# Typed graph attention: GpSimd builds the one-hots of the weighted sums, and one stage divides, turns and projects

## The reference, cut to what matters

```python
def _L1_gnn_ref(h, ..., a_linears, ..., skip, node_type, etype, row_idx, col_idx):
    ...
    ex = jnp.exp(score - m[col_idx])
    denom = jax.ops.segment_sum(ex, col_idx, num_segments=n)
    alpha = ex / denom[col_idx]
    agg = jax.ops.segment_sum(alpha[..., None] * msg_edge, col_idx, num_segments=n)
    agg = agg.reshape(n, OUT_DIM)
    out = _typed_matmul(agg, a_linears, node_type)
    out = jax.nn.sigmoid(skip)[node_type][:, None] * out
    return out
...
x = x + _L1_gnn_ref(_layernorm(x, axis=-1), ...)
```

## Time and profile before

| | |
|---|---|
| median of three runs | 5765.59 us |
| the profiled execution's span | 6191.8 us |
| `build_counts`, 536.4 to 870.1 | 333.7 us |
| `edge_weights`, 3168.1 to 3272.4 | 104.3 us |
| `edge_sums`, 3274.8 to 3503.7 | 228.9 us |
| division, to the end of its stage, 3503.7 to 3513.6 | 9.9 us |
| turn and loading, 3513.6 to 3528.4 | 14.8 us |
| four projections, 3528.4 to 3624.9 | 96.5 us |

### The profile page before, as it was taken

The page is one execution under the profiler, slowest core; times in us unless marked ns, Lnnn a source line. Parts: engine busy times, 40 slices in busy tenths (PEclk is TensorE's granted clock), DMA queues, the critical chain, the costliest instruction groups (busy, mean ns, idle before and its releaser), DMA issues. The chain is left out here.

```text
span 6191.8 us, 76002 instructions
## 1 busy us (share of the span) xinstructions
PE 4533.9 (73%) x22806; PEld 3190.3 (52%) x22842; DVE 3374.5 (55%) x7236; ACT 1645.9 (27%) x3766; POOL 2414.1 (39%) x2719
## 2 busy tenths in 40 slices
PE   5877978757758694566558889998999495354468
PEld 1223434545546452444436677777888363344456
DVE  8988972645556654677757743342111333544454
ACT  0964652411213251011100133333222121100022
POOL 0851018545540534555500028861122301577710
PEclk8988989868878897666758989999999697677779
DMA  0002447422232388777746410004333332233310
GB/s 31 2 11 102 190 181 210 157 45 39 41 60 79 100 322 277 236 246 240 242 132 218 149 25 12 17 7 129 100 110 120 91 100 61 91 91 90 92 29 21
DMA packets 413215, 696.03 MB, mean 112 GB/s; under 512 B 116843, under 2 KB 301299, under 8 KB 408203
## 3 DMA queue, kind: packets, MB, share of 16 engines
q1 hardware_dynamic: 316322, 440.23, 22.7%
q0 software_dynamic: 96320, 250.79, 13.5%
q10 hardware_dynamic: 192, 0.15, 0.0%
HBM read 450.69 MB, written 239.64 MB: 111 GB/s over the span
## 5 line engine op out<-in xcount | busy, mean ns | idle before, releaser
L1109 PE MATMUL wsum_a_ps<-wsum_a_hot,wsum_a_rows 128*128 128x128 f32 x1664 | 290.4, 349 | 359.7 <-DVE big L1136 185.7
L2242 POOL DMA_INDIRECT big<-hgt_table,edge_key x416 | 394.2, 948 | 364.4 <-DVE hgt_s_tmp L2335 221.0
L1095 POOL DMA_INDIRECT wsum_a_rows<-table,edge_src x416 | 434.2, 1044 | 221.9 <-issue 165.5
L1109 PEld LDWEIGHTS wsum_a_ps<-wsum_a_hot,wsum_a_rows 128*128 128x128 f32 x1664 | 272.1, 257 | 378.0 <-issue 210.0
L3928 PE MATMUL sagel_ps<-sagel_piece,sagel_high 128*128 128x448 f32 x1050 | 399.0, 380 | 0.8 <-issue 0.8
L3928 PE MATMUL sagel_ps<-sagel_piece,sagel_low 128*128 128x448 f32 x1050 | 385.2, 367 | 0.0
L2325 DVE TENSOR_REDUCE hgt_highest<-hgt_s_pm 128x8 f32<-128x1024 f32 x208 | 253.3, 1219 | 188.3 <-remote 181.6
L2242 POOL DMA_INDIRECT big<-gat_table,own_src x288 | 272.5, 946 | 211.6 <-issue 82.0
L2292 PE MATMUL hgt_s_pq<-big 128*128 x1248 | 249.9, 372 | 136.0 <-DVE hgt_s_tmp L2335 75.6
L2282 PE MATMUL hgt_s_pm<-hgt_s_turned,pick 112*128 112x128 bf16 x1664 | 188.5, 282 | 216.9 <-DVE hgt_highest L2325 185.3
L790 PE MATMUL cnt_ps<-cnt_hot_s,cnt_hot_d 128*128 128x512 bf16 (+1 forms) x1724 | 309.8, 333 | 39.0 <-DVE cnt_hot_s L772 34.9
(11 more groups left out here) (1007 smaller groups left out, 10909.7 us busy)
## 6 DMA issues: line engine op xcount, KB each, us to landing
hgt_edge_values<-big SPq DMA_DIRECT2D x104, 512.0 KB
big<-hgt_edge_values SPq DMA_DIRECT2D x104, 512.0 KB, 4.6
x<-counts SPq DMA_DIRECT2D x75, 448.0 KB, 3.3
x<-counts SPq DMA_DIRECT2D x75, 336.0 KB, 2.9
counts<-big SPq DMA_DIRECT2D x25, 832.0 KB, 3.4
counts<-big SPq DMA_DIRECT2D x25, 768.0 KB, 3.3
big<-counts SPq DMA_DIRECT2D x30, 640.0 KB
counts_turned<-big SPq DMA_DIRECT2D x30, 640.0 KB
```

Source lines behind the costliest of these rows:

```text
L1095: nc.gpsimd.indirect_dma_start(rows[n % DEEP][:, u, :], None, table, bass.IndirectOffsetOnAxis(ap=e.src[:, g:g + 1], axis=0)).then_inc(gat ...
L1109: mm = nc.tensor.matmul(ps[r.slot % 2][u][:, k * P:(k + 1) * P], rows[r.slot][:, u, k * P:(k + 1) * P], hot[r.slot % 2][:, u, :], start=Tr ...
L2242: nc.gpsimd.indirect_dma_start(rows[n % DEEP][:, u, :], None, at.table, bass.IndirectOffsetOnAxis(ap=at.index[:, g:g + 1], axis=0)).then_i ...
```

## The change

- `edge_sums`: GpSimd builds the one-hots, one operation of 128x128 for each group (416 in all, L2964 of the new kernel) in a buffer that is free at that time. `hot` and `val` have three places. VectorE only copies the weights (L2981) and multiplies (L2983). The load of `w_a` is issued by SyncE behind the fifth step's rows.
- `typed_out` takes the place of `divide`, `turn`, the load and the four `add_projection`. It goes tile by tile: VectorE multiplies by the reciprocal (L3046), TensorE transposes (L3082), ScalarE copies out, TensorE multiplies by all four matrices (L3094), VectorE adds the four types' parts (L3061) and takes the statistics (L3065).
- `edge_weights`: three places in place of two for `hot_t` and `pd`, and one-hots made two batches ahead.
- `not_below_zero`: a bitwise AND of a register before each wait on its value, in `build_counts` (440 on VectorE, 50 on ScalarE) and `edge_sums` (416 on TensorE, 25 on ScalarE).

```diff
+def not_below_zero(value, highest):
+    return value & ((1 << highest.bit_length()) - 1)
...
@@ build_counts, VectorE @@
-                            dve.wait_ge(moved, buckets[u] + 1)
+                            dve.wait_ge(moved, not_below_zero(buckets[u], 2 * NT - 1) + 1)
...
@@ edge_weights @@
+        pd = [c.enter_context(nc.psum_tensor(f"{nm}_pd{a}", [P, 512], F32)) for a in range(RING)]
...
-                    if b >= 2:
-                        dve.wait_ge(spread, b - 1)
+                    if b >= RING:
+                        dve.wait_ge(spread, b - RING + 1)
...
                 make(0)
+                make(1)
                 for b in range(batches):
-                    if b + 1 < batches:
-                        make(b + 1)
+                    if b + 2 < batches:
+                        make(b + 2)
...
@@ edge_sums @@
-        val, hot = many(2, "val", [P, R, W]), many(2, "hot", [P, R, P])
+        PLACES = 3
+        val = many(PLACES, "val", [P, R, W])
+        hot = [at.spare[1][:, k * R * P:(k + 1) * R * P].rearrange("p (r n) -> p r n", r=R) for k in range(PLACES)]
...
                     sp.dma_start(rows[n % DEEP], at.put_by[:, n * R:(n + 1) * R, :]).then_inc(loaded[n % DEEP], 16)
+                    if n == DEEP:
+                        for to, what in loads:
+                            sp.dma_start(to, what).then_inc(brought, 16)
+                sp.wait_ge(brought, 16 * len(loads))
+
+            @block.gpsimd
+            def _(pool):
+                for n in range(steps):
+                    if n >= PLACES:
+                        pool.wait_ge(done, (n - PLACES + 1) * R + BASE)
+                    for u in range(R):
+                        nc.gpsimd.tensor_scalar(hot[n % PLACES][:, u, :], kit.iota[:], e.rec[:, n * R + u, 1:2], None,
+                                                ALU.is_equal).then_inc(matched, 1)
...
-                        dve.wait_ge(done, n * R + BASE - R)
-                        nc.vector.tensor_tensor(hot[k % 2][:], kit.iota[:, None, :].broadcast_to([P, R, P]),
-                                                e.rec[:, ds(n * R, R), 1:2].broadcast_to([P, R, P]), ALU.is_equal
-                                                ).then_inc(matched, 1)
+                        if n >= PLACES:
+                            dve.wait_ge(done, (n - PLACES + 1) * R + BASE)
...
-                        pe.wait_ge(matched, n + 1)
+                        pe.wait_ge(matched, (n + 1) * R)
...
-                            pe.wait_ge(moved, blocks[u] + 1)
+                            pe.wait_ge(moved, not_below_zero(blocks[u], NT - 1) + 1)
...
+def typed_out(nc, kit, nm, acc, H, w, is_kind, skip, x):
+    TYPES, DK = is_kind.shape[1], (acc.shape[2] - H) // H
+    with ExitStack() as c:
+        def many(count, name, shape):
+            return [c.enter_context(nc.sbuf_tensor(f"{nm}_{name}{a}", shape, F32)) for a in range(count)]
+        plain, st = many(2, "plain", [P, D]), many(3, "st", [P, 2, P])
+        pt = [c.enter_context(nc.psum_tensor(f"{nm}_pt{u}", [P, 512], F32)) for u in range(2)]
+        po = [c.enter_context(nc.psum_tensor(f"{nm}_po{u}", [P, TYPES * D], F32)) for u in range(2)]
+        step, normed, turned, kept, multiplied, added, measured = sems(
+            nc, c, nm, "step normed turned kept multiplied added measured")
+        with nc.Block() as block:
+            @block.vector
+            def _(dve):
+                link = link_on(dve, step)
+                link(nc.vector.tensor_scalar(acc[:, :, 0:H], acc[:, :, 0:H], 1e-30, None, ALU.max))
+                link(nc.vector.reciprocal(acc[:, :, 0:H], acc[:, :, 0:H]))
+                def norm(t):
+                    if t >= 2:
+                        dve.wait_ge(turned, t - 1)
+                    nc.vector.tensor_tensor(plain[t % 2][:].rearrange("p (h d) -> p h d", h=H),
+                                            acc[:, t, H:].rearrange("p (h d) -> p h d", h=H),
+                                            acc[:, t, 0:H][:, :, None].broadcast_to([P, H, DK]), ALU.mult
+                                            ).then_inc(normed, 1)
+                norm(0)
+                norm(1)
+                for k in range(TYPES):
+                    link(nc.vector.tensor_scalar(is_kind[:, k, :], is_kind[:, k, :], skip[:, k:k + 1], None, ALU.mult))
+                for t in range(NT):
+                    if t + 2 < NT:
+                        norm(t + 2)
+                    dve.wait_ge(multiplied, t + 1)
+                    for k in range(TYPES):
+                        if k:
+                            dve.wait_ge(added, t * TYPES + k)
+                        nc.vector.scalar_tensor_tensor(out=nat(x)[:, t, :], in0=po[t % 2][:, k * D:(k + 1) * D],
+                                                       scalar=is_kind[:, k, t:t + 1], in1=nat(x)[:, t, :],
+                                                       op0=ALU.mult, op1=ALU.add).then_inc(added, 1)
+                    dve.wait_ge(added, (t + 1) * TYPES)
+                    nc.vector.bn_stats(kit.stats[:, t, :], nat(x)[:, t, :]).then_inc(measured, 1)
+            @block.scalar
+            def _(act):
+                for t in range(NT):
+                    act.wait_ge(turned, t + 1)
+                    if t >= 3:
+                        act.wait_ge(multiplied, t - 2)
+                    nc.scalar.copy(st[t % 3][:], pt[t % 2][:, 0:D].rearrange("p (k n) -> p k n", k=2)).then_inc(kept, 1)
+            @block.tensor
+            def _(pe):
+                def turn_tile(t):
+                    pe.wait_ge(normed, t + 1)
+                    if t >= 2:
+                        pe.wait_ge(kept, t - 1)
+                    for k in range(2):
+                        mm = nc.tensor.transpose(pt[t % 2][:, k * P:(k + 1) * P], plain[t % 2][:, k * P:(k + 1) * P],
+                                                 kit.ident[:])
+                    mm.then_inc(turned, 1)
+                turn_tile(0)
+                for t in range(NT):
+                    if t + 1 < NT:
+                        turn_tile(t + 1)
+                    pe.wait_ge(kept, t + 1)
+                    if t >= 2:
+                        pe.wait_ge(added, (t - 1) * TYPES)
+                    for k in range(TYPES):
+                        for q in range(2):
+                            mm = nc.tensor.matmul(po[t % 2][:, k * D:(k + 1) * D], st[t % 3][:, q, :], w[:, 2 * k + q, :],
+                                                  start=(q == 0), stop=(q == 1))
+                    mm.then_inc(multiplied, 1)
```

More of the change, by code:

```diff
@@ L2572, in edge_weights @@
         ends, hot_t = ([at.spare[0][:, a * size:(a + 1) * size].bitcast(BF16) for a in places]
-                       for places in (range(RING), range(RING, RING + 2)))
+                       for places in (range(RING), range(RING, 2 * RING)))
         high = many(2, "high", [P, B, H])
-        pd = [c.enter_context(nc.psum_tensor(f"{nm}_pd{a}", [P, 512], F32)) for a in range(2)]
+        pd = [c.enter_context(nc.psum_tensor(f"{nm}_pd{a}", [P, 512], F32)) for a in range(RING)]
         pd_v = [p[:, 0:B * 3 * H].rearrange("p (g k h) -> p g k h", k=3, h=H) for p in pd]
@@ L2910, in finish, with edge_sums @@
             sp.wait_ge(self.stored[u], 16 * sum(u < self.tiles(m) for m in range(self.spans)))
-def edge_sums(nc, kit, nm, at, weights, acc):
+def edge_sums(nc, kit, nm, at, weights, acc, loads):
     e, H, dv = at.edges, at.heads, at.dv
@@ L2934, in edge_sums @@
         ps = c.enter_context(nc.psum_tensor(f"{nm}_ps", [P, 2 * REGION], F32))
-        ready, matched, weighed, valued, done, moved, copied = sems(
-            nc, c, nm, "ready matched weighed valued done moved copied")
+        ready, matched, weighed, valued, done, moved, copied, brought = sems(
+            nc, c, nm, "ready matched weighed valued done moved copied brought")
         loaded = gather_sems(nc, nm, "loaded", DEEP)
@@ L2982, in _ @@
                         for u in range(R):
[L2984 to L2985 removed]
+                            pe.wait_ge(moved, not_below_zero(blocks[u], NT - 1) + 1)
+                            nc.tensor.matmul(ps[:, ds(regions[u], W)], hot[n % PLACES][:, u, :], val[n % PLACES][:, u, :],
                                              start=False, stop=False, skip_group_check=True).then_inc(done, 1)
@@ L3370, in hgt_stage @@
             acc = cc.enter_context(nc.sbuf_tensor("hgt_acc", [P, NT, H + D], F32))
-            edge_sums(nc, kit, "hgt_a", at, scores, acc[:])
-            def divide(link):
-                link(nc.vector.tensor_scalar(acc[:, :, 0:H], acc[:, :, 0:H], 1e-30, None, ALU.max))
-                link(nc.vector.reciprocal(acc[:, :, 0:H], acc[:, :, 0:H]))
-                link(nc.vector.tensor_tensor(nat(b1).rearrange("p t (h d) -> p t h d", h=H),
-                                             acc[:, :, H:].rearrange("p t (h d) -> p t h d", h=H),
```

(12 more changed lines are left out.)

20 lines of the change are left out of this document (10 added, 10 removed).

## The result

The changed kernel takes 5850.47 us, the median of four runs (5848.81 to 5851.75), against 5763.22 (four runs, 5760.42 to 5766.13) for the kernel before on the same chip: a ratio of 1.0147, 95% interval 1.0136 to 1.0159. The prediction was 5737 with a range of 5712 to 5815 and 0.53 for faster; the measured time lies 35 us above the range.

The account below looks back on a forecast made before the run. In the sums a two-place loop between VectorE and TensorE set the step, TensorE's 2.06 just under it. Sums -10.4, behind them -22.7, register operations +4 made -29 from 5765.6: 5737 us, range 5712 to 5815.

Parts of the forecast that it names:

- The price of a one-hot on GpSimd: In the sums: p, the us one GpSimd one-hot holds, taken as 0.20; step 2.07 against 2.17, -10.4 us.
- The high end: Upper bound of p in the sums from L2157's 2.52 ns a column: 0.323 with fixed part hidden, 0.565 if not.
- the pair of constants written 0.03 apart: Two operations lasting 0.10 each start 0.03 apart, read as the fixed part hiding behind the operation ahead.
- Turns on the shared path: In the sums, VectorE's product and GpSimd's four one-hots take turns: step = 1.21 + 4p, 2.01 at p = 0.20.
- The rule of the Trainium skill: GpSimd near line rate with one input, twice VectorE's time with two; for the sums it would give -10.4 us.
- The bound of 2.06 on TensorE: In the sums, TensorE's own 2.06 us a step ends last, so the step was put at 2.07.
- the extra register operations there: One more per group on TensorE's queue in the sums, 0.04 us each: at most 0.16 a step, +6 for -10.4.
- Unless TensorE's step also holds waiting that I can't see: In the sums, if TensorE's 2.06 hides waiting, its eight records make 1.75: -44 us at best.
- Behind the sums: The merged tile-by-tile stage after the sums ends at 3602.1 against 3624.88: -22.7 us, bounds -27 to -10.
- The edge counts: An AND of 0.04 us before each of 440 VectorE waits, 110 of them exposed: +4 us, between 0 and 18.
- The third place in the weights: In the weights no engine is full, so a third place is worth 0, a gain of up to 3.
- The rival on the other side: One-hots in the sums at L2157's 2.52 ns a column: fixed part hidden 2.50, 5781 us, 0.18; unhidden 3.47, 5882, 0.09.

## Why the prediction was wrong, point by point

- **The price of a one-hot on GpSimd** is the step that failed. I wrote "I take p = 0.20, half of the CAST's fixed part hidden"; by the starts it is 0.58 alone, almost nothing hidden, at 2.66 ns a column. The high end was in the text: L2157 with nothing hidden, p = 0.565, and I gave it 0.09 and left it out of the range. Two readings led away from it. The first was the layout: I put L2157's rate down to its gaps, because a MEMSET with the same gaps is slow. The new one-hots have none and cost the same, so the rate wasn't the layout's. What the two share is the operation, a `tensor_scalar` that compares; no run has another operation in that form, so whether it is the comparison that costs stays open. (A scalar for each partition is in the new one-hots alone: L2157 compares with a constant.) A row with the same operation should have weighed more than one with the same layout. The second was the pair of constants written 0.03 apart, from which I took that the fixed part hides; between the one-hots only 0.02 of it does (0.580 from start to start, 0.599 long).
- **Turns on the shared path**: "step = 1.21 + 4p" has a wrong size, and its form holds for this product only. Turns are taken, but over a part of the one-hot: a product of 1.22 us costs the one-hots 0.89, one of 0.41 costs them nothing. VectorE pays a little, in its copy (168 ns before, 259 now). With p = 0.58 and 0.89 the formula gives 3.21, where the trace has 3.20; with my 1.21 it would have given 3.53.
- **The rule of the Trainium skill** (GPSIMD Engine Reference, section 4.1, Engine selection), stated there for elementwise add, multiply and maximum, that GpSimd runs near line rate with one input, doesn't carry over to these one-hots: 2.66 ns a column, as for L2157, against 0.83 for the CAST. The measurement decides.
- **The bound of 2.06 on TensorE, and the extra register operations there**: "could lengthen the step by 0.16 at most". In the changed kernel they cost next to nothing, since GpSimd is later. But there was more behind them than I allowed: with VectorE's one-hots each takes 0.095 us of the queue, and four 0.38. "Unless TensorE's step also holds waiting that I can't see" was right: with one wait and one AND in place of four the step goes to 1.81.
- **Behind the sums**: -22.7 predicted, -22.9 measured. The first product comes 2.98 us into the stage (predicted 3.0), the tiles stand 3.67 apart (predicted 3.72), VectorE's share stays hidden, the granted clock is 0.98.
- **The edge counts**: +4 predicted, +4.3 measured. Four visits together take 40 ns longer, and 27 of them stand ahead of the first, as predicted in the main. **The third place in the weights**: 0 predicted; the stage takes 97.8 us before and 97.7 after, from the first to the last operation on its tiles. **The load of the matrices** beside the sums shows in no wait.
- **The rival on the other side** was the one that came: the one-hot on GpSimd is slow, and it decided from a step of 2.35; the measured 3.2 lies between its two cases, 2.50 and 3.47. Its price is that of the second (0.58 against 0.565); that the time is 5850 and not that case's 5882 comes from the turn, which was 0.89 and not 1.21.

## What to carry to other kernels

Price a moved operation by the rows of the same operation on the engine it moves to, even where type and layout differ, and ask of a row with a friendlier price whether it does the same work. Beside an engine that shares its path, add the standstill to the price, and look first whether the slower engine alone already passes the step, as here: 4 x 0.58 = 2.32 against 2.15. A register operation that a queue can't hide can cost more than its record, here 0.095 us and not 0.036; where an engine's idle time says "issue", count its register operations and waits before giving it another place in the ring.

## What the runs showed of the hardware that I had not expected

- The standstill is nearly one-sided: in all runs VectorE's product kept 1.21 to 1.27 us in the mean, while the one-hot that met it grew by 0.79 to 0.97. VectorE's small copy ahead of it grew from 0.168 to 0.259 us, and to 0.295 in the run with the quarter of the product. In the kernel before, a VectorE operation of 0.166 us had taken 13.29 beside a GpSimd operation of 13.67; here VectorE never waited so, with GpSimd's operations of 0.58 in the way.
- The two exclude each other in a part of the GpSimd operation only. With 128 columns a long one-hot ends 0.469 us after the product that it met, of 0.598 that it lasts alone; with 64 columns 0.307 of 0.437; with a constant 0.386 of 0.527. Reckoned back from these ends, it came to a stand 0.13 to 0.14 us after its start each time. A product of 0.41 us that begins 0.30 us into a one-hot makes no standstill at all.
- With a constant an operation showed 72 ns less and its starts were 27 ns further apart. Why is open.
